# Six extra TensorE matmuls per batch in the second edge walk of a graph, attention and expert kernel

## The reference

```
xn = layernorm(x)
h  = layernorm(xn) * ln_w + ln_b
h  = elu(gat(h, W1, att_src1, att_dst1, 8 heads of 64) + b1)      # walk one
g  = gat(h, W2, att_src2, att_dst2, 1 head of 256) + b2            # walk two
m  = rmsnorm(linear_attention(rmsnorm(xn)) @ w_out + b_out) + xn   # mixing, 4 heads of 32
x  = x + g + m
x  = x + expert_ffn(layernorm(x))                                  # 8 experts, top 1, capacity 977
```

## Time and profile before

| | |
|---|---|
| median of three runs | 3825.99 us (3814.42 to 3826.52) |
| the profiled execution, its span | 3820.3 us |
| PE busy | 2906.2 us, 76% of the span |
| DVE busy | 2350.6 us, 62% |
| POOL busy | 1807.1 us, 47% |
| ACT busy | 1407.6 us, 37% |
| mean granted TensorE clock | 0.858 of full speed |

### The profile page before, as it was taken

One profiled execution on the slowest core, in us unless ns is written; L12 is line 12 of the kernel. 1 busy time (PEld: TensorE's weight loads), 2 busy tenths in 40 slices (PEclk: granted clock), 3 DMA queues, 4 the chain that ended last, 5 costly groups with the idle time before them and its releaser, 6 DMA issues. The chain is left out here.

```text
span 3820.3 us, 71476 instructions
## 1 busy us (share of the span) xinstructions
PE 2906.2 (76%) x16525; PEld 2210.8 (58%) x16526; DVE 2350.6 (62%) x7735; ACT 1407.6 (37%) x5084; POOL 1807.1 (47%) x1891
## 2 busy tenths in 40 slices
PE   8587877778877788885677766576676666689998
PEld 6466656566656666674555555455555544657666
DVE  6776666666667667685555554456666666735445
ACT  5544444444444444432222222133333321333432
POOL 0355555555555555502555555555555555411111
PEclk9798998999899998997778877777777777599999
DMA  5455555555555555512444543533222232421220
GB/s 190 128 161 157 160 159 161 156 157 162 159 158 157 159 162 157 148 38 86 110 109 115 145 129 81 151 84 83 80 79 80 80 81 73 146 88 50 78 87 12
DMA packets 208914, 454.46 MB, mean 119 GB/s; under 512 B 46680, under 2 KB 112803, under 8 KB 208682
## 3 DMA queue, kind: packets, MB, share of 16 engines
q0 software_dynamic: 118128, 361.70, 34.8%
q1 hardware_dynamic: 76030, 76.73, 6.5%
q10 hardware_dynamic: 14524, 13.40, 1.0%
HBM read 406.27 MB, written 49.35 MB: 119 GB/s over the span
## 5 line engine op out<-in xcount | busy, mean ns | idle before, releaser
L1272 POOL DMA_INDIRECT weights<-table,w_idx x880 | 842.1, 957 | 749.8 <-issue 283.2
L778 POOL DMA_INDIRECT w_G<-table,w_idx x880 | 839.8, 954 | 694.4 <-PE PS L911 296.7
L911 PE MATMUL PS<-w_G,w_S 128*128 128x260 f32 x3520 | 976.7, 425 | 80.1 <-DVE ACC L1000 54.2
L911 PEld LDWEIGHTS PS<-w_G,w_S 128*128 128x128 f32 x3520 | 694.0, 208 | 200.3 <-issue 69.6
L1479 PE MATMUL PS<-weights 128*128 128x257 f32 x1760 | 606.7, 485 | 253.5 <-DVE ACC L1676 134.7
L1479 PEld LDWEIGHTS PS<-weights 128*128 128x128 f32 x1760 | 390.2, 243 | 370.6 <-issue 244.7
L1000 DVE TENSOR_TENSOR ACC<-ACC,PS 128x520 f32 x464 | 321.1, 692 | 254.0 <-PE PS L911 211.0
L988 DVE TENSOR_TENSOR w_G<-w_G,PS 128x512 f32<-128x512 f32 x660 | 431.9, 682 | 32.3 <-ACT PS L807 11.9
L820 ACT ACTIVATE w_G<-w_G 128x64 f32<-128x64 f32 x1760 | 441.4, 335 | 0.0
L1676 DVE TENSOR_TENSOR ACC<-ACC,PS 128x257 f32 x464 | 196.2, 423 | 321.2 <-remote 110.9
L1300 ACT ACTIVATE w_PW<-w_Z 128x4 f32<-128x4 f32 x220 | 45.2, 206 | 925.6 <-DVE w_Z L1661 733.8
(11 more groups left out here) (326 smaller groups left out, 3826.7 us busy)
## 6 DMA issues: line engine op xcount, KB each, us to landing
weights<-in_L_ffn_w SPq DMA_DIRECT2D x16, 1024.0 KB, 7.8
w_G<-table,w_idx POOLq DMA_INDIRECT x880
weights<-table,w_idx POOLq DMA_INDIRECT x880
table<-ACC SPq DMA_DIRECT2D x49, 260.0 KB
xbuf<-XR SPq DMA_DIRECT2D x8, 1040.0 KB
XR<-xbuf SPq DMA_DIRECT2D x7, 1040.0 KB, 5.3
table<-row ACTq DMA_DIRECT2D x49, 129.0 KB, 2.2
weights<-table SPq DMA_DIRECT2D x49, 129.0 KB
```

The source lines that it names most:

```text
L778: pool.indirect_dma_start(G[:, r, b, :], None, table, IndexOn(ap=idx[:, r, b:b + 1], axis=0)).then_inc(fetched[r], 16)
L911: last = pe.matmul(PS[:, 2 * j + a, 0:W // layer.banks], lhsT, rhs, start=b == slots[0], stop=b == slots[-1])
L1272: pool.indirect_dma_start(G[:, r, b, :], None, table, IndexOn(ap=idx[:, r, b:b + 1], axis=0)).then_inc(fetched[r], 16)
```

## The change

A function `busy` is added and called once in each step of PE, between the spreading and the turning. It issues six bfloat16 matmuls with 256 moving columns each. They read `ST` of the batch that was just spread, and write columns 256 to 511 of the PSUM bank 4 or 5, which nothing reads. No wait and no semaphore is added. Since `step` is called for 217 of the 220 batches, 1302 matmuls are added, each with a weight load of its own.

```diff
                 last.then_inc(summed, 1)
 
+            def busy(r):
+                for i in range(6):
+                    pe.matmul(PS[:, 4 + r % 2, 256:512], ST[:, r % 2, i % B, :], ST[:, r % 2, 0:2, :].rearrange("p b e -> p (b e)"), start=True, stop=True)
+
             def step(b, mixing=None, a=None):
                 n, r, h = b.n, b.slot(RING), b.slot(HOT)
                 t, mine = tiles_of(pe, b.back(-2)), steps_of(b)
                 for step_ in mine[:len(mine) // 2]:
                     sum_up(n, r, *step_)
                 spread_nodes(b.back(-2), t)
+                busy(r)
                 turn(n + 3, (r + 3) % RING, (h + 3) % HOT)
```

## The result

The changed kernel takes 3845.34 us (median of 4 runs, 3842.65 to 3848.15), the kernel before takes 3821.01 us (4 runs, 3814.42 to 3826.52) in the same comparison. The ratio is 1.0064, with a 95% interval of 1.0049 to 1.0078: slower by over 0.3%. The forecast was 3861 us, slower.

The account below looks back on a forecast made before the run. Walk two was taken as bound by the time around a closed ring of sums, fetch and logits, not TensorE's throughput. 0.5 x 60 + 5 = +35 us on 3820.3, plus 5.7 from span to median, gave 3861 us; range 3795 to 3925.

Parts of the forecast that it names:

- TensorE's added time: Walk two, net on TensorE: 160 us of added matmuls less 100 us given back, 60 us more.
- The filler's own length: Six added matmuls per batch: 0.66 us at 2.4 GHz, 1.32 at 1.2 GHz; 12% cold, 160 us in all.
- What the clock gives back: Walk two's sums and turning: half of 205 us of cold time goes, 100 us.
- walk one's cold share: 10% of walk one's sums run at the low clock; used as a guide to walk two with the added work.
- The share that reaches the end: Walk two: 0.5 of TensorE's added time lengthens the kernel; its waits for copy and merges hide the other half.
- natural experiment: Walk two's stretches and walk one compared: batch time rises by 0.61 or 0.37 of TensorE's added time; 0.5 taken.
- its own test: The share of 0.5 is wrong if TensorE's busy time per batch rises over 0.4 us and the batch doesn't.
- The standstills: Walk two: pauses of 5 us, expected in the same number after the change.
- The extra code: PE's matmuls and loads rise 21%; waits on the sums might grow 22 us, 5 us put into the sum.
- The clock rival: Walk two stays near 2.4 GHz, all 205 us of cold time go: -38 us, 3788 us; chance 0.2.
- The cover rival: Walk two: the matmuls run wholly in TensorE's existing waits, POOL's cadence sets the batch: 3826 us; chance 0.2.
- The full-price rival: Walk two: each batch waits for the sums' second half, nothing given back: +178 us, or +109 at share 0.61; chance 0.1.

Follow-up runs that it names:

- the repeat: The changed kernel, unedited, against the kernel before on one more chip of the first kind: 3843.79 against 3816.56 us, ratio 1.0069.
- twelve: Changed kernel with 12 added matmuls per batch, not six, between spreading and turning, against the kernel before, first kind of chip: 3865.09 us, ratio 1.0130.
- the end of the step: Added matmuls moved behind the second half of the sums, against the kernel before, second kind of chip: 0.9985 and 0.9992 with six, 1.0005 with 12.
- the constants: Walk two's tile number fixed, not loaded, against the kernel before, second kind of chip: 0.9975 and 0.9971; with the six matmuls too, 0.9982.

## Why the prediction was right, and where its sizes were not

The direction and the mechanism held: a part of the filler is given back by the clock, a part of the rest reaches the end. The sum forecast +35 us and +24 to +27 was measured. But the two main factors were each off by about two, in opposite senses: TensorE's added time was some 100 to 109 us and not 60, and the share of it that reached the end about a quarter and not a half. That their product came out near is in part luck.

**The filler's own length** held at either clock, but not in the mixture. At the high clock six matmuls last from 2421.42 to the turning at 2422.08, 0.66 us as worked out; at the low clock from 2428.02 to 2429.26, 1.24 us for 1.32.

```profile
2421.42 0.82 PE L1484 MATMUL PS<-w_ST 128*128 128x256 bf16 x6
...
2422.08 0.39 PE L1458 MATMUL PS<-w_ident,weights 128*128 128x128 bf16 x4
...
2428.02 1.44 PE L1484 MATMUL PS<-w_ST 128*128 128x256 bf16 x6
...
2429.26 0.63 PE L1458 MATMUL PS<-w_ident,weights 128*128 128x128 bf16 x4
```

The weight loads cost nothing, as put. Over all 217 steps the time from the first added matmul to the turning is 176 us (188 in the repeat), where 160 was forecast with 12% of them cold. It is 0.81 us a step, so (0.81 - 0.66) / (1.24 - 0.66) = 26% are cold, more than of the sums.

**What the clock gives back** was over-sized. Expected: 100 of 205 us. The sums gave (485 - 447) x 1760 = 67 us (in the repeat 487 to 438 ns, 86 us), the turning nothing. The reason given, walk one's cold share of 10%, was too hopeful: (447 - 383) / 414 = 15% of the sums are still cold. Clock 0.84 and 447 ns lie within or near the 0.82 to 0.87 and 435 that were named. The net is then 176 - 67 = 109 us more for TensorE, not 60 (in the repeat 188 - 86 = 102). The busy sums say the same, taken per batch because the fixed stretch holds 857 gathers before and 848 after: 980.86 x 4 / 857 = 4.58 us and 1077.28 x 4 / 848 = 5.08 us, which over 217 batches is 109 us (99 in the repeat).

**The share that reaches the end** was over-sized too: 24.3 of 109 us is 0.22, in the repeat 27.2 of 99 is 0.27, not 0.5. The stretches looked like a natural experiment, but between them DVE's, ACT's and PE's work changes together. They were also read coarsely: by batch numbers the batches near the end take 6.33 us and not 6.15. The prediction named its own test (TensorE's time per batch rises by over 0.4 us and the batch doesn't). The keys stretch comes nearest to it, +0.34 us against +0.01, in the repeat +0.41 against +0.06. The other stretches pay, 0.14 to 0.27 us a batch.

What the trace shows in place of the even share is that the batches have two rhythms on this kind of chip: a run of gathers without a pause, and a batch with a wait of at least 1.5 us. The filler turns batches without a pause into batches with a short wait, and shortens the long standstills. It does so in all stretches, keys too: there 10, 22 and 16 of 48 batches (none, short, long) became 3, 40 and 5. But in keys what is gained and what is lost cancel (100.6 and 101.0 us of waits), while in the queries stretch the waits rise from 189.2 to 205.6 us. Why they cancel in one and not in the other stays open. By the prediction's division 7.05 us was expected for keys and 6.91 measured, for queries 6.75 and 6.73.

**The standstills** of over 5 us were expected in the same number and fell from 24 to 4 (24 to 8 in the repeat), the clearest miss. That they were slack, which TensorE's own lateness now takes up, is a reading and not shown.

**The extra code** was put at 5 us and measures 1 to 3 us on the second kind of chip; on the first it was not measured.

**The rivals.** The clock rival is refuted twice: six give 0.84, and twelve, which do bring 0.91 and 409 ns, cost 1.3%. The cold time was there to be had, but it wasn't worth the path. The Trainium skill's rule ("TensorE: Matmul & The Clock Gate", "What's actually happening") that activity releases the throttle agrees with the granted clock, 0.78, 0.84, 0.91 for none, six, twelve; it says nothing of who waits. The cover rival, 3826 us, is refuted on the first kind of chip by both intervals, and holds on the second where the filler stands at the end of the step. The full-price rival is refuted: 24 us is far from its 109 and 178.

**What stays open.** Whether the end of the step removes the loss on the first kind of chip too: all three such kernels fell on the second. What the filler delays that matters, the turning or the second half of the sums. What sets the two kinds apart. And what ends a wait on the first kind about 1 us behind POOL's last gather, for four engines within a microsecond; the constants were to test one answer and could not.

## What to carry to other kernels

A warmer TensorE pays only if TensorE bounds the end: read who waits for whom before buying clock. If work is added for its own sake, try it behind the instructions that the other engines wait for; on the second kind of chip the place alone was worth 13.4 us, 0.43%. A list of who waited for whom may count plain spacing as waiting, so look at the length of one wait before adding them up. And a share read between two stretches of the same loop is not a price as long as several engines' work differs between them.

## What was not expected of the hardware

The same program takes some 3816 us on one kind of chip and 3091 on another, 23% more, and the verdict on the change is of the same sign but half the size (0.64 and 0.69% against 0.33%). An indirect gather's row is the same on both, 0.95 us with 0.30 us ahead of it. On the first kind a wait ahead of a batch's fetch is 0.3 us or at least about 1.5, hardly ever between, so it seems that a few hundred nanoseconds on TensorE are either free or cost a whole wait.
